# One layer of graph aggregation, linear attention and routed delta-rule memory: two placement constants of the vector engine's row loop, 7 and 8, become 5 and 7

## The chip, the cores and the metric

One core of a Trainium2 chip runs the whole layer. The metric is the device time of one execution in microseconds (us), lower is better. Engines are named as in the profile: PE (TensorE), DVE (VectorE), ACT (ScalarE), POOL (GpSimd) and SP (SyncE, which here only issues DMAs).

## The reference, cut to what matters

The layer adds a graph convolution and a linear attention to x (1250 tokens x 512), and then a third part, to which the change belongs. It sends each token to two of four experts and runs a gated delta-rule recurrence over each expert's tokens:

```
scores = softmax(h @ Wgate); rw, sel = top_k(scores, 2)     # 4 experts
q = l2norm(silu(h @ Wq)); k = l2norm(silu(h @ Wk)); v = silu(h @ Wv)   # 8 heads x 64
beta = sigmoid(h @ Wb)
g = -exp(A_log) * softplus(h @ Wa + dt_bias)
# per expert, over its tokens in order:
S = S * exp(g_t); kv = k_t S; delta = (v_t - kv) * beta_t
S = S + k_t (x) delta;  o_t = (q_t * scale) S
core = sum over the two experts of rw * o
out = (rmsnorm(core) * silu(h @ Wg)) @ Wo
```

## The kernel before, in words

Tokens are cut into 10 tiles of 125 (`NT = 10`). Each token takes part twice, which makes 2500 slots, padded to 2560 and cut into 40 chunks of 64; two chunks are one unit of the recurrence (20 units). The change lies in the stage before the recurrence, the feature stage, from some 380 to 510 us of the trace. What happens there, engine by engine, each in the order of its own program:

- **PE** projects each token tile three times, for q, k and v (`project_rows(t, w)`, w = 0, 1, 2, L783; 8 matmul instructions a projection), t from 0 to 9. Before projection (t, w) it waits until ACT has taken (t-1, w) out of the same bank. After the three projections of tile `DECAY_AT` it runs `decay_sums()` (L827 to L834): three transposes and two sums over the gates `gbg`, for which it waits on `gb_ready`. After tile 9 come the gate projections of tiles 1 to 4 (w = 3), then `features(0)` (L869), the first transposes of the recurrence, which wait for q and k rows of unit 0 from memory; then `head_gate(5)` (L994).
- **ACT** takes each projection out with SiLU (L1128 for w = 0 and 1, L1130 for w = 2). Behind (t+1, 0) it takes the square roots of tile t (`row_norms`, L1171), for which it waits on `ss_done` from DVE. SiLU, Sqrt and Exp each need a table load when they follow one another. After tile `DECAY_AT` it runs `decays()` (L1157 to L1167), the exponentials of what `decay_sums()` made.
- **DVE** runs the loop over tiles that the constants belong to. `squares(t)` (L1903 to L1905) waits for ACT's (t, 1), and sets `ss_done`; `unit_rows(t)` (L1911 to L1914) waits for the square roots and for (t, 2), and sets `rows_done`. After tile `GAMMA_AT` comes `gates_in()` (L1877 to L1885): it waits on `gb_loaded`, copies the gates into `gbg` (which sets `gb_ready`) and beta into `bet`. After tile `DECAY_AT` comes `decay_rows()` (L1887 to L1894), which turns ACT's exponentials into `stepT`, `gamT` and `bdec`, and sets `rows_made` and `scal_done`.
- **POOL** sends 20 scatters of the gates to `gb_slots` (L1385), then two scatters for each tile of q, k and v rows to `qkv_slots` (L1391), each behind `rows_done` of its tile. A row is 6144 bytes.
- **SP** waits until all gate scatters have landed, loads the gates back as `gbp` (L454, two DMAs; each row of a chunk is 64 bytes), then waits on `rows_made`, writes `stepT` and `gamT` to memory (L458, L459), waits until they have landed, and issues eight loads from them for units 0 and 1 (L465). Only then does it wait for the last row scatters and issue the loads of q and k for units 0 and 1 (L481).

`gb_loaded` reaches its 32 when both loads of `gbp` have landed in full.

Of the kernel before, what the change touches and what calls it, by code (L numbers as in the profile page):

```python
# [46 lines left out]
LB = NT // 2  # L47
GROUPS = ((0, 5), (5, 10), (0, 4), (4, 8), (8, 10))
XR = 112
GAMMA_AT = 7  # L50
DECAY_AT = 8
EARLY = 5
LATE = 7
ROOTS_BEHIND = {(2, 2): 0, (3, 0): 1, (3, 2): 2, **{(t, 0): t - 1 for t in range(4, NT)}}
# [48 lines left out]
def gps_layer(nc, d, out):  # L103
# [5 lines left out]
    with ctx:  # L109
# [430 lines left out]
        def _(pe):  # L540
# [233 lines left out]
            def project_rows(t, w, tiles=()):  # L774
                b0 = feature_bank(t, w)
                if w < 3 and t:
                    pe.wait_ge(S["f_act"], feature_count(t - 1, w))
                if w == 3 and 1 <= t < 4:
                    pe.wait_ge(S["f_act"], feature_count(NT - 1, t - 1))
                if w == 3 and t >= 4:  # L780
                    pe.wait_ge(S["f_act"], feature_count(t - 4, 3))
                for k in range(KC):
                    last = mm(bank[:, b0, :], xT[:, k, t * P:t * P + 128], W[:, w, k, :], start=(k == 0), stop=(k == KC - 1))  # L783
                    if k == KC - 1:
                        last.then_inc(S["f_psum"], 1)
                    if tiles:
                        for i in range(2):
                            small = token_logits(tiles[k // 2], k % 2 * 2 + i)
                if NT - 1 in tiles:
                    small.then_inc(S["logit_psum"], 1)  # L790
# [36 lines left out]
            def decay_sums():  # L827
                pe.wait_ge(S["gb_ready"], 1)
                for g in range(3):
                    c0, c1 = 16 * g, min(16 * g + 16, NCK)  # L830
                    last = nc.tensor.transpose(bank[0:(c1 - c0) * H, 6, g * CL:(g + 1) * CL], gbg[0:CL, c0 * H:c1 * H], ident[0:CL, 0:CL])
                last.then_inc(S["decay_psum"], 1)
                mm(bank[:, 7, 0:NCK * H], later, gbg[:, :], start=True, stop=True)
                mm(bank[:, 0, 0:NCK * H], alike, gbg[:, :], start=True, stop=True).then_inc(S["decay_psum"], 1)  # L834

            for t in range(2, NT):
                for w in range(3):
                    project_rows(t, w)
                if t == DECAY_AT:
                    decay_sums()  # L840
# [223 lines left out]
        def _(act):  # L1064
# [92 lines left out]
            def decays():  # L1157
                act.wait_ge(S["decay_psum"], 1)
                act.wait_ge(S["step_exp"], 1)
                A(stepT[:, 0:2, :], bank[:, 6, 0:2 * CL].rearrange("p (g n) -> p g n", g=2), ACT.Exp)  # L1160
                A(stepT[0:64, 2, :], bank[0:64, 6, 2 * CL:3 * CL], ACT.Exp).then_inc(S["step_exp"], 1)
                act.wait_ge(S["decay_psum"], 2)
                for b0, to in ((7, bdec), (0, gtot)):
                    for b in range(2):
                        q = slice(CL * b, CL * b + CL)
                        last = A(to[q, :, :], bank[q, b0, 0:NCK * H].rearrange("p (c b j) -> p b c j", b=2, j=HB)[:, b], ACT.Exp)
                last.then_inc(S["decay_exp"], 1)  # L1167

            def row_norms(t):
                act.wait_ge(S["ss_done"], t + 1)  # L1170
                A(nrm[:, t % 4, :], nrm[:, t % 4, :], ACT.Sqrt).then_inc(S["rn_done"], 1)  # L1171
# [6 lines left out]
            for t in range(2, NT):  # L1178
                for w in range(3):
                    feature_rows(t, w)  # L1180
                    if (t, w) in ROOTS_BEHIND:
                        row_norms(ROOTS_BEHIND[t, w])
                if t == DECAY_AT:
                    decays()
# [315 lines left out]
        def _(dve):  # L1500
# [375 lines left out]
            def gates_in():  # L1876
                dve.wait_ge(S["gb_loaded"], 32)  # L1877
                for b in range(2):
                    last = V.tensor_copy(gbg[:, :].rearrange("p (c b j) -> p b c j", b=2, j=HB)[:, b],
                                         gbp[:, :, 0:H].rearrange("p c (j b) -> p b c j", b=2)[:, b])  # L1880
                last.then_inc(S["gb_ready"], 1)
                for b in range(2):
                    q = slice(CL * b, CL * b + CL)
                    step(V.tensor_copy(bet[q, :, :], gbp[q, :, H:2 * H].rearrange("p c (j b) -> p b c j", b=2)[:, b]))
                step(V.memset(headT[:, :, :], 0.0))  # L1885

            def decay_rows():  # L1887
                dve.wait_ge(S["step_exp"], 2)
                step(V.tensor_copy(headT[:, :, 0:1], stepT[:, :, 0:1]))
                V.memset(stepT[:, :, 0:1], 0.0).then_inc(S["rows_made"], 1)  # L1890
                dve.wait_ge(S["rows_made"], 1)
                V.tensor_tensor_scan(flat(gamT), flat(stepT), flat(headT), 0.0, ALU.mult, ALU.add).then_inc(S["rows_made"], 1)
                dve.wait_ge(S["decay_exp"], 1)
                V.tensor_tensor(bdec[:, :, :], bdec[:, :, :], bet[:, :, :], ALU.mult).then_inc(S["scal_done"], 1)  # L1894
# [12 lines left out]
            def unit_rows(t):  # L1907
                b = t % 4
                qk = row_tile(t)[:, 0:2 * D]
                dve.wait_ge(S["rn_done"], t + 1)  # L1910
                step(V.reciprocal(nrm[:, b, :], nrm[:, b, :]))  # L1911
                V.scalar_tensor_tensor(tt3(qk[:, 0:D]), tt3(qk[:, 0:D]), DH ** -0.5, bc(nrm[:, b, 0:H], DH), ALU.mult, ALU.mult)
                dve.wait_ge(S["f_act"], feature_count(t, 2))
                V.tensor_tensor(tt3(qk[:, D:2 * D]), tt3(qk[:, D:2 * D]), bc(nrm[:, b, H:2 * H], DH), ALU.mult).then_inc(S["rows_done"], 1)  # L1914
# [5 lines left out]
            for t in range(NT):  # L1920
                squares(t)
                unit_rows(t)
                if t == GAMMA_AT:
                    gates_in()
                if t == DECAY_AT:
                    decay_rows()
# [175 lines left out]
```

## Time and profile before

| | us |
|---|---|
| median of 3 runs | 882.66 (880.85 to 884.09) |
| the profiled execution, its own time | 880.85 |
| its span in the trace | 879.0 |
| PE busy | 811.3 (92%) |
| DVE busy | 641.8 (73%) |
| POOL busy | 340.4 (39%) |
| ACT busy | 311.7 (35%) |

The span runs from the first to the last instruction; 1.85 us of the profiled execution lie around it. All starts in the rows are microseconds from the span's start. A share of busy time is an average over stages with different limits, so what bounds one stage is read from the engines' timelines and the chain of waits in that stage.

### The profile page before, as it was taken

The page shows a single profiled execution, that of the slowest core. Times are in us where ns is not written, and L with a number is a line of the kernel's source. Part 1 is how long each engine was busy: PE and PEld are TensorE (multiplying, and loading weights), DVE is VectorE, ACT ScalarE, POOL GpSimd, SP SyncE. Part 2 cuts the span into 40 slices and gives each one's busy share as a digit, 9 for nine tenths or more (in the row PEclk, how much of TensorE's full clock was granted, in tenths as well). Part 3 has the DMA queues.
Part 4 walks back from the last instruction along what each step waited for, and adds up shares of the span by engine and source line. Part 5 has one row for each costly group of instructions (what it writes and reads, how often), then busy time and mean ns, then how long its engine had stood idle before and what let it go on. Part 6 is the DMA issues. An engine that isn't in the chain of part 4 may idle for free.

```text
span 879.0 us, 23079 instructions
## 1 busy us (share of the span) xinstructions
PE 811.3 (92%) x9754; PEld 546.6 (62%) x9754; DVE 641.8 (73%) x1345; ACT 311.7 (35%) x548; POOL 340.4 (39%) x300
## 2 busy tenths in 40 slices
PE   2998999999999999999999978999999999997698
PEld 2454444344566657765444447989889898887343
DVE  7999999986888755526844437888887877783385
ACT  1231112210222220033645533555556465553352
POOL 5221110000111140000772346878767777771550
PEclk9999999999999989999999998999999999999899
DMA  8500000031000034000059544454544544421462
GB/s 253 185 1 1 0 2 1 1 72 46 2 1 1 2 114 150 0 1 1 5 198 387 194 128 112 120 151 125 140 128 133 148 132 135 124 56 40 120 178 70
DMA packets 74958, 80.42 MB, mean 91 GB/s; under 512 B 34452, under 2 KB 57670, under 8 KB 74853
## 3 DMA queue, kind: packets, MB, share of 16 engines
q1 hardware_dynamic: 69733, 57.78, 23.5%
q0 software_dynamic: 5120, 21.14, 6.7%
q8 instruction: 79, 1.29, 0.6%
q14 instruction: 26, 0.21, 0.1%
HBM read 54.44 MB, written 24.39 MB: 90 GB/s over the span
## 4 chain that ended last, share of the span: by engine, by line
PE 69%; DVE 23%; issue 3%; DMA 2%; POOL 1%; ACT 1%; SPq 1%; DVEq 0%; POOLq 0%; ACTq 0%
PE bank L783 12%; PE bank L852 8%; PE bank L878 4%; PE bank L1051 4%; PE bank L593 4%; DVE rows L1551 4%; PE bank L579 4%; PE bank L904 3%; DVE rows L1553 3%; PE bank L799 3%; DVE rows L1680 3%; PE bank L800 3%; PE bank L952 3%; PE bank L939 2%; PE bank L869 2%
## 5 line engine op out<-in xcount | busy, mean ns | idle before, releaser
L783 PE MATMUL bank<-W,xT 128*128 128x512 f32 x280 | 124.0, 596 | 0.0
L783 PEld LDWEIGHTS bank<-W,xT 128*128 128x128 f32 x280 | 52.0, 190 | 59.3 <-issue 58.4
L1371 POOL TENSOR_TENSOR cnt_r<-cnt_r,ident_sb 125x125 fp32r<-125x125 f32 x10 | 11.4, 1139 | 173.9 <-ACT cnt_r L1116 173.9
L557 PE MATMUL bank<-W,xT 128*125 128x512 f32 x160 | 77.1, 596 | 0.0
L579 PEld LDWEIGHTS bank<-rows 128*126 128x126 f16 x360 | 43.5, 135 | 34.7 <-issue 24.2
L1686 DVE TENSOR_SCALAR rows<-iota_sb,tC 128x625 f16<-128x625 f16 x180 | 56.2, 378 | 10.5 <-PE bank L579 10.5
L579 PE MATMUL bank<-rows 128*126 128x313 f16 x360 | 58.9, 299 | 4.2 <-DVE rows L1686 4.1
L1551 DVE TENSOR_SCALAR rows<-iota_sb,gbp 125x180 f16<-125x180 f16 x160 | 56.3, 352 | 0.0
L1553 DVE TENSOR_SCALAR rows<-iota_sb,gbp 125x180 f16<-125x180 f16 x160 | 50.4, 315 | 0.0
L567 PE MATMUL bank<-rows 125*128 125x360 f16 x160 | 42.7, 318 | 5.7 <-DVE rows L1553 3.3
L852 PE MATMUL bank<-big 64*64 64x64 f32 (+1 forms) x1280 | 43.8, 212 | 3.1 <-issue 2.0
L557 PEld LDWEIGHTS bank<-W,xT 128*125 128x125 f32 x160 | 28.9, 190 | 25.6 <-issue 25.0
L799 PE MATMUL bank<-hs_high,cnt_r 125*125 125x512 f32 x100 | 42.6, 426 | 1.3 <-DVE hs_r L1788 1.3
L1220 ACT ACTIVATE tB<-bank 128x1024 f16<-128x1024 f32 x40 | 40.9, 1023 | 7.1 <-PE bank L904 5.4
L646 PE MATMUL bank<-xT,W 128*128 128x500 f32 (+1 forms) x96 | 42.1, 520 | 1.3 <-ACT W L1105 0.7
L567 PEld LDWEIGHTS bank<-rows 125*128 125x128 f16 x160 | 15.4, 96 | 43.9 <-DVE rows L1553 29.3
L976 PE MATMUL bank<-state,W 64*64 64x64 f32 x640 | 42.1, 224 | 0.1
L980 PE MATMUL bank<-tC,W 64*64 64x64 f32 x640 | 41.0, 221 | 0.4 <-issue 0.4
L712 PE MATMUL bank<-W,xT 128*125 128x512 f32 x80 | 40.8, 591 | 0.0
L852 PEld LDWEIGHTS bank<-big 64*64 64x64 f32 (+1 forms) x1280 | 39.0, 128 | 2.8 <-issue 1.8
L800 PE MATMUL bank<-hs_r,cnt_r 125*125 125x512 f32 x100 | 40.3, 403 | 0.0
L1070 ACT ACTIVATE xT<-bank 128x500 f32<-128x500 f32 x20 | 11.0, 587 | 82.1 <-PE bank L551 82.1
(338 smaller groups left out, 1976.8 us busy)
## 6 DMA issues: line engine op xcount, KB each, us to landing
big<-qkv_slots SPq DMA_DIRECT2D x40, 256.0 KB, 3.5
rows<-step_rows SPq DMA_DIRECT2D x40, 128.0 KB, 3.2
rows<-gam_rows SPq DMA_DIRECT2D x40, 128.0 KB, 3.3
big<-qkv_slots SPq DMA_DIRECT2D x80, 64.0 KB, 2.8
big<-qkv_slots SPq DMA_DIRECT2D x40, 128.0 KB, 2.9
o_slots<-big SPq DMA_DIRECT2D x40, 128.0 KB, 2.8
x_all<-in_x SPq DMA_DIRECT2D x10, 224.0 KB
out<-tC SPq DMA_DIRECT2D x10, 224.0 KB
```

The lines of the kernel that those rows point to most:

```text
L557: last = mm(dst, xT[:, k, t * P:(t + 1) * P], W[:, w, k, :], start=(k == 0), stop=(k == KC - 1 and bias is None))
L567: mm(bank[:, 7, 0:2 * SW], oh_row[:, i // SB % SR, i % SB, :], oh_col[:, i % (SR * SB), :, :].rearrange("p a n -> p (a n)"), start=False, ...
L579: last = mm(bank[0:OW, b0 + k, 0:n], oh_src[:, g % 2, j, :], oh_dst[:, i % WB, t0:t0 + n], start=(j == 0), stop=(j == SC - 1))
L646: last = mm(bank[:, u % 2, 0:n], W[:, 2, k, c * 128:(c + 1) * 128], xT[:, k, t0:t0 + n], start=(k == 0), stop=(k == KC - 1))
L783: last = mm(bank[:, b0, :], xT[:, k, t * P:t * P + 128], W[:, w, k, :], start=(k == 0), stop=(k == KC - 1))
L799: mm(bank[0:P, t % 2, :], cnt12[:, s, t * P:(t + 1) * P], hs_high[:, s, :], start=(s == 0), stop=False)
L800: last = mm(bank[0:P, t % 2, :], cnt12[:, s, t * P:(t + 1) * P], hs_low[:, s, :], start=False, stop=(s == NT - 1))
L852: last = mm(bank[q, b0, a * CL:(a + 1) * CL], lhsT[q, a, :], rhs[q, a, :], start=start(a), stop=True, skip_group_check=not start(1))
L976: mm(bank[q, DB, o0 + j * DH:o0 + (j + 1) * DH], qG[u // 2 % 2][u % 2][q, c2 * HB + j, :], state[q, c % 2, j, :], start=True, stop=False)
L1551: V.tensor_scalar(oh_col[:, i % (SR * SB), 0, :], iota[0:P, 0:SW], e_col[:, i:i + 1], e_src[:, i:i + 1], ALU.is_equal, ALU.mult)
L1553: V.tensor_scalar(oh_col[:, i % (SR * SB), 1, :], iota[0:P, 0:SW], e_col[:, i:i + 1], e_dst[:, i:i + 1], ALU.is_equal, ALU.mult).then_inc( ...
L1686: V.tensor_scalar(oh_dst[:, i % WB, :], iota[:, 0:HN], srt[:, 1, i:i + 1], None, ALU.is_equal).then_inc(S["onehots_done"], 1)
```

## The change

Two constants. `gates_in()` on DVE moves from behind tile 7 to behind tile 5. `decay_sums()` on PE, `decays()` on ACT and `decay_rows()` on DVE, which share the other constant, move from behind tile 8 to behind tile 7. Nothing is added or removed.

```diff
-GAMMA_AT = 7
-DECAY_AT = 8
+GAMMA_AT = 5
+DECAY_AT = 7
```

## Rows read from the trace of the kernel before

**Rows 1.** Chain of waits, 380 to 560 us: start us, duration us, what, count.
```profile
408.88 72.25 PE bank L783 x168
481.13 0.32 PE bank L831 x3
...
482.73 10.31 PE bank L783 x24
...
498.34 6.39 DMA qkv_slots<-big,posi
...
505.19 4.76 DMA big<-qkv_slots
...
510.08 1.64 PE bank L869 x8
```

**Rows 2.** Timeline of DVE: start us, duration us, engine, line, operation.
```profile
456.68 0.68 DVE L1914 TENSOR_TENSOR big<-big,nrm 128x512 f32<-128x512 f32 x1
...
477.96 0.39 DVE L1879 COPY gbg<-gbp 128x160 f32<-128x160 f32 x2
...
479.12 1.23 DVE L1903 TENSOR_TENSOR tB<-big 128x1024 f32<-128x1024 f32 x1
...
481.64 0.17 DVE L1905 TENSOR_SCALAR nrm<-nrm 128x16 f32<-128x16 f32 x1
```

**Rows 3.** Timeline of SP, the DMAs it issues.
```profile
449.12 5.07 SPq L454 DMA_DIRECT2D gbp<-gb_slots  x2
490.83 0.41 SPq L458 DMA_DIRECT2D step_rows<-stepT  x1
...
497.28 3.43 SPq L465 DMA_DIRECT2D rows<-step_rows  x4
```

**Rows 4.** DMA queues, 448 to 454.6 us: packets, MB, share of 16 engines.
```profile
q1 hardware_dynamic: 2565, 0.16, 26.7%
```

**Rows 5.** DMA queues, 454.6 to 474 us.
```profile
q0 software_dynamic: 1450, 7.93, 98.7%
q1 hardware_dynamic: 1232, 0.08, 4.4%
```

**Rows 6.** DMA queues, 474 to 475.5 us.
```profile
q0 software_dynamic: 76, 0.37, 63.1%
q1 hardware_dynamic: 1036, 0.07, 47.4%
```

**Rows 7.** DMA queues, 475.5 to 477 us.
```profile
q1 hardware_dynamic: 319, 0.02, 14.6%
```

**Rows 8.** DMA queues, 477 to 484.5 us.
```profile
q0 software_dynamic: 452, 2.43, 79.3%
```

**Rows 9.** Timeline of POOL: the first scatter of tile 6, the second of tile 7.
```profile
470.99 0.95 POOL L1391 DMA_INDIRECT qkv_slots<-big,posi  x1 [7.48 <-DVE big L1914]
...
479.62 1.55 POOL L1391 DMA_INDIRECT qkv_slots<-big,posi  x1 [0.30 <-issue]
```

**Rows 10.** Timeline of ACT, tile 7's root to projection (8, 1).
```profile
476.21 0.22 ACT L1171 ACTIVATE nrm<-nrm 128x16 f32<-128x16 f32 x1
476.44 1.28 ACT L1128 ACT_TABLE_LOAD   x1
477.74 0.60 ACT L1128 ACTIVATE big<-bank 128x512 f32<-128x512 f32 x1
...
484.60 1.28 ACT L1128 ACT_TABLE_LOAD   x1
```

**Rows 11.** Timeline of PE: both head gates.
```profile
511.51 4.75 PE L994 MATMUL bank<-W,xT 128*128 128x512 f32 x8
...
517.88 3.60 PE L994 MATMUL bank<-W,xT 128*128 128x512 f32 x8
```

**Rows 12.** Busy by window: us, each engine's busy (instructions), PEclk, DMA share, GB/s.
```profile
484.00:490.00 6.00, 6.00 (x16) 2.65 (x15) 1.61 (x4) 5.59 (x8) 0.00 (x0) 1.00 0.00 0
...
511.50:516.30 4.80, 4.80 (x12) 2.18 (x11) 0.00 (x0) 1.09 (x3) 3.87 (x3) 0.76 0.02 3
```

## The prediction

> **What bounds the kernel now.** I read the chain of waits first. From 408.88 us it stays on PE through 21 projections without a gap (168 matmuls in 72.25 us, 3.44 us a projection), then `decay_sums()` from 481.13, then the last three projections from 482.73 to 493.04 [rows 1]. So the feature stage is bound by PE, and whatever makes PE wait there is paid in full. Behind it the chain leaves PE: ACT takes (9, 2) out, tile 9's roots and rows follow, POOL issues the last scatter at 498.34, it lands 6.39 us later, the q and k loads take 4.76 us, and at 510.08 the recurrence begins [rows 1]. That tail hangs on the end of projection (9, 2), so a shift of 493.04 shifts the start of the recurrence, and all behind it, by nearly the same.
>
> Second, the timeline of DVE, to see what room each moved piece has. `unit_rows(5)` ends at 457.36, `gates_in()` starts at 477.96 [rows 2]. The change moves `gates_in()` to 457.4: some 20 us earlier, in an engine that runs its program in order.
>
> Third, because `gates_in()` waits for a DMA, the DMA queues over time. SP issues both loads of `gbp` from 449.12 to 454.19 and nothing more until 490.83 [rows 3], so every packet of the hardware queue in between is theirs. 2565 of them go by 454.6 [rows 4]; then only 1232 in 19.4 us, beside 1450 packets of the software queue that carry 7.93 MB and keep the 16 engines 98.7% busy [rows 5]. These are POOL's row scatters for tiles 0 to 5, two a tile, issued before 463.5 [rows 9]. At 474 they run out: 1036 small packets go in 1.5 us, the last 319 before 477.0, and none after it [rows 6 to 8]. The sum is 5152, both loads. The second load, of 160 KB, therefore takes from 454 to about 477, because it shares each engine nearly packet by packet with 6 KB packets. It landed less than 1 us before DVE asked for it at 477.96. The place of `gates_in()` is just late enough in the kernel before.
>
> **The change part by part.**
>
> *Work moved.* `gates_in()` takes 1.16 us (477.96 to 479.12) [rows 2], `decay_sums()` 1.60 us (481.13 to 482.73) [rows 1], `decays()` on ACT 2.8 us (from the end of taking out (8, 2), 481.13 + 0.02 + 0.60, to the SiLU table load at 484.60) [rows 1, 10]. All run once before and once after, with the same table loads: 0 by themselves. No DMA is added.
>
> *The new wait.* Call T the time at which `gb_loaded` is complete. The loads are issued at the same time as before and meet the same 12 scatters, whose issue ended 7.48 us ahead of 470.99 [rows 9]. Tile 6's scatters, which began at 470.99 and so took part of the last 3 us, now come behind `gates_in()`, so T can come a little earlier: bounds 475.5 and 477.0 [rows 6, 7], and I take 476.0. DVE stands from 457.4 to 476.0, 18.6 us. Behind the wait on DVE are `squares(6)`, `unit_rows(6)` and all later tiles; ACT waits for `ss_done` of tile 6 at its root, in front of (7, 1); PE waits for `gb_ready` after (7, 2), which it ends at 481.13 less three projections, 470.81.
>
> *When PE can start (8, 1).* Two paths. Through ACT: T, `gates_in()` 1.16, `squares(6)` 2.69 (479.12 to 481.81) [rows 2], 0.2 to pass it on, root 0.23, SiLU table 1.28, taking out (7, 1) 0.60 [rows 10]: T + 6.2. Through PE: `gbg` copied at T + 0.4, `decay_sums()` 1.60, projection (8, 0) 3.44: T + 5.4 at full clock. PE will have stood idle for 5.6 us. The only like case near it: after PE's idle time before 510.08 the granted clock was 0.76 over 511.5 to 516.3 [rows 12], part at full (2.4 GHz) and part at half (1.2 GHz); the eight transposes there took 1.64 us [rows 1] and eight matmuls 4.75, against 3.60 later for the same eight [rows 11]. The matmuls alone lost 1.15; scaling the transposes by the same share gives 0.4 to 0.6 more. So the clock costs 0 to 1.7 and I take 1.7, as this idle time is longer: T + 7.1, which is 483.1. The Trainium skill, TensorE: Matmul & The Clock Gate, section "What's actually happening", has the engine at 1.2 GHz once it has stood idle, which speaks for the full loss; a stall in the middle of the projections, where this matters, no row here shows. If the clock stayed up, the path through ACT would decide, and the sum would be 0.9 less.
>
> *From there.* Before, (8, 1) started at 481.13 - 2 x 3.44 = 474.25. After it come five projections in the changed kernel, 17.2 us, with `decay_sums()` already done: 483.1 + 17.2 = 500.3 for the end of (9, 2), against 493.04: +7.3. ACT keeps up on the same durations: (7, 2) is out at about 482.8 and PE needs it at 486.5; `decays()` ends at 485.6, then a SiLU table and (8, 0) to 487.5, needed at 490.0; root 7 between two table loads, then (8, 1) to 490.9, needed at 493.4.
>
> *What comes late next.* `decay_rows()` now waits for `unit_rows(7)`, which hangs on root 7 at 488.9, so `rows_made` comes at about 491.5, against 490.83 when SP saw it before [rows 3]: no earlier, though its place is one tile earlier. SP issues the eight row loads from some 498 to 505, as before [rows 3], while the last scatter is issued at 498.34 + 7.3 = 505.6. So these loads no longer run beside the last scatter. It took 6.39 us [rows 1]; one with no other traffic, issued at 479.62, was done by 484.5 [rows 8, 9, 12], 4.9. The relief is 0 to 1.5 there, 0 to 0.5 on the q and k loads; I take 1.1 together. PE's four gate projections end at 500.3 + 13.8 = 514.1, ahead of `features(0)` at 510.1 + 6.2 = 516.3.
>
> *Sum.* +7.3 - 1.1 = +6.2 us. On the profiled execution's own time 880.85 + 6.2 = 887.1 (its span 885.2, with 1.85 around it). The median of the runs shown is 1.8 above that execution, so the forecast for a median is 882.7 + 6.2 = 888.9. The mechanism's own bounds: T at 475.5, no clock loss, full relief: 475.5 + 6.2 + 17.2 = 498.9, +5.9 - 2.0 = +3.9, and a further 1.4 off if the shorter idle time before `features(0)` leaves the clock up: +2.5. At the top T at 477.0, clock loss, no relief: +8.3.
>
> **The rivals.**
>
> *A, the load is there early and the earlier decays pay (faster).* If T were 469.7 or less, PE would find `gbg` and (7, 1) in time (470.81 + 1.60 + 3.44 = 475.85, less 6.2): that is the point from which it decides. Then `rows_made` comes at about 480, the writes and the eight row loads are done before the last scatter, which lands in 4.9 instead of 6.39 us, and the q and k loads gain up to 0.5: -2.0, and -1.0 more if PE, idle for 1.3 us instead of 3.3, keeps its clock: about -3.0, 879.7. For it: the first load went at some 500 packets a microsecond [rows 4]. Against it: the second at 64 [rows 5], in the very traffic that stays. The Trainium skill, DMA: Bandwidth & Descriptors, section "Queues, rings and completion order", has an engine drain a whole packet of some 9 to 17 descriptors from one ring before it turns to another. With nine small ones to each large one, T would be some 3 us after 454.6 and this rival would win; the rows count 1232 against 1450, about one to one, and they decide. 5%.
>
> *B, the wait is there but swallowed (no change).* PE is idle before 510.08 for 3.3 us, and a pause in the middle could be made up there. For it: that idle time, and the lighter DMA traffic behind it. Against it: the idle time is the end of a chain that itself starts at (9, 2), so it moves with the stall; only relief and clock, 3.4 at most, come off. If also the path through PE cost less than I think: +2, 884.7. 12%.
>
> *C, the stall is dearer.* Tiles 6 and 7 now scatter at 483 and 491 and the last three tiles' traffic is as dense as before; if the load in 475.5 to 477 is not helped, T at 477.0 (+1.0), the clock low for twice as long (+1.7), and nothing relieved (7.3 in place of 6.2): +10, 892.7. 8%.
>
> **How the numbers follow.** The forecast has 75%. A measurement of this kernel can tell about 0.5% (4.4 us) from no change. In the forecast's own case the shift is over 4.4 in five of six, which with C gives 0.71 for slower; B, the low end of the forecast's case and a little of A give 0.24 for the same; A the rest, 0.05. The range from 884.0 (+1.3, most of B) to 892.0 (+9.3, part of C) leaves out A and the rest of C, some 15% with the spread of the runs, 3.2 us, on top.
>
> **What would show it right or wrong.** Right: DVE idle for 18 to 20 us before L1879, released by the DMA of `gbp`, which starts there near 476; PE idle for 5 to 6 us before L831 near 476.5; the granted clock low for a few microseconds from there; (9, 2) taken out at about 500; the last scatter shorter than 6.39 us; `features(0)` at about 516. Wrong: L1879 starting before 470 (A), or PE's gap small; `features(0)` within 2 us of 510 (B); the clock loss missing takes 0.9 off. If the hardware queue's 64-byte packets between 454.6 and 474 are not near 1200 again, my reading of how the load shares the engines is wrong.

## The result and the profile after

The changed kernel takes 887.43 us in the median of 5 (887.12 to 888.31), the kernel before 882.42 (880.85 to 884.09; two executions more than were shown before the prediction). The ratio is 1.0069, with a 95% interval of 1.0044 to 1.0095; it is not the quotient of the two medians (1.0057). How it was formed isn't recorded; over all 24 executions on record of the changed kernel the median is 887.58 and the quotient of the means 1.0070. So the changed kernel is slower by 5 us going by the medians and by 6 going by the ratio (3.9 to 8.4): under 1%, but clear of the noise. 888.9 had been forecast.

The timeline of DVE in the changed kernel answers to [rows 2]: start, duration, engine, line, operation, and in brackets the idle time before it and what ended that.

```profile
456.80 0.68 DVE L1914 TENSOR_TENSOR big<-big,nrm 128x512 f32<-128x512 f32 x1
476.42 0.40 DVE L1879 COPY gbg<-gbp 128x160 f32<-128x160 f32 x2 [18.93 <-DMA gbp<-gb_slots]
...
477.59 1.23 DVE L1903 TENSOR_TENSOR tB<-big 128x1024 f32<-128x1024 f32 x1
...
480.10 0.17 DVE L1905 TENSOR_SCALAR nrm<-nrm 128x16 f32<-128x16 f32 x1
```

DVE stands still for 18.93 us, and the load of `gbp` ends that. The DMA queues from 454.6 to 474 us show the same traffic as [rows 5]: packets, MB, share of 16 engines.

```profile
q0 software_dynamic: 1459, 7.98, 99.1%
q1 hardware_dynamic: 1205, 0.08, 4.3%
```

The timeline of PE shows its stall, and the windows below it the clock (busy time and instructions of each engine, PEclk as a share of 2.4 GHz, DMA share, GB/s):

```profile
439.81 31.06 PE L783 MATMUL bank<-W,xT 128*128 128x512 f32 x72
476.87 0.58 PE L831 MATMUL bank<-ident_sb,gbg 64*128 64x64 f32 x3 [5.99 <-DVE gbg L1879]
...
479.67 35.88 PE L783 MATMUL bank<-W,xT 128*128 128x512 f32 x80
516.23 1.10 PE L869 MATMUL bank<-ident_sb,big 128*128 128x128 f32 x8 [0.69 <-ACT hs L1133]
517.16 3.60 PE L994 MATMUL bank<-W,xT 128*128 128x512 f32 x8
```

```profile
470.90:476.80 5.90, 0.00 (x0) 0.00 (x0) 0.38 (x3) 0.00 (x0) 0.00 (x0) 0.90 0.84 287
476.80:482.40 5.60, 5.53 (x11) 3.03 (x12) 4.78 (x10) 2.06 (x4) 0.00 (x0) 0.50 0.00 0
482.40:488.10 5.70, 5.70 (x15) 2.59 (x14) 2.62 (x3) 5.59 (x12) 1.90 (x2) 1.00 0.69 276
```

PE idles 5.99 us. The clock is full up to 475.6, in the middle of the idle time, and 0.50, which is 1.2 GHz, from there to 482.4. ACT and POOL, for the end of the stage:

```profile
481.84 0.60 ACT L1128 ACTIVATE big<-bank 128x512 f32<-128x512 f32 x1
...
501.85 0.60 ACT L1130 ACTIVATE big<-bank 128x512 f32<-128x512 f32 x1 [2.83 <-PE bank L783]
...
515.58 0.60 ACT L1133 ACTIVATE hs<-bank 125x512 f32<-125x512 f32 x1 [2.84 <-PE bank L783]
```

```profile
507.12 0.95 POOL L1391 DMA_INDIRECT qkv_slots<-big,posi  x1 [0.30 <-issue]
```

(9, 2) is taken out at 501.85, 8.8 us later than 493.04 [rows 1], `features(0)` starts at 516.23, 6.15 later, and it is no longer held by a DMA but by PE's own gate projections and ACT behind them (L1133). Last, SP:

```profile
449.23 5.04 SPq L454 DMA_DIRECT2D gbp<-gb_slots  x2
491.67 0.41 SPq L458 DMA_DIRECT2D step_rows<-stepT  x1
...
512.28 1.77 SPq L481 DMA_DIRECT2D big<-qkv_slots  x4
```

`rows_made` comes 0.84 us later than before [rows 3], although its place is one tile earlier. The last scatter is over when SP goes on, 512.28 - 507.12 = 5.2 us after its issue, against 6.39 [rows 1].

**A measure for the rest.** Executions of one kernel start this stage up to 1.8 us apart, and their recurrences differ by more. So I compare profiled executions by the time from SP's issue of L454 to PE's first key product (L878, the first work of the recurrence that needs all of unit 0's features): "stage" below. Before: 516.10 - 449.12 = 67.0 us (PE's L878 starts at 516.10). After: 520.60 - 449.23 = 71.4, +4.4. The rest of the trace, L878 to the first L1051, took 317.9 us in the profiled execution before and 322.2 in the one after; over the 14 profiled executions of this case it lies anywhere from 317.9 to 324.1. That is why the profiled execution after (890.02 us) is 9.2 us above the one before while the medians are 5.0 apart. The same kernel in e7 has 319.1, so most of it is spread between executions; whether the change also adds a little there is not shown.

### The profile page after: what moved, and what is told of

It reads as the page before. It is cut to its first block, busy times and chain, and to the rows that moved or that the text cites. A ratio compares the mean times of both kernels' runs of the same rounds, so it can differ in the third digit from the quotient of the medians.

```text
span 888.2 us, 23079 instructions
## 1 busy us (share of the span) xinstructions
PE 813.3 (92%) x9754; PEld 548.2 (62%) x9754; DVE 643.9 (72%) x1345; ACT 312.0 (35%) x548; POOL 339.9 (38%) x300
## 4 chain that ended last, share of the span: by engine, by line
PE 62%; DVE 23%; issue 5%; DMA 4%; POOL 4%; ACT 1%; SPq 1%; DVEq 0%; POOLq 0%; ACTq 0%
PE bank L852 8%; PE bank L783 6%; PE bank L878 4%; PE bank L1051 4%; PE bank L579 4%; DVE rows L1551 3%; PE bank L904 3%; PE bank L593 3%; DMA gbp<-gb_slots 3%; PE bank L799 3%; DVE rows L1680 3%; PE bank L952 3%; DVE rows L1553 3%; PE bank L800 3%; PE bank L939 2%
## 5 line engine op out<-in xcount | busy, mean ns | idle before, releaser
L852 PE MATMUL bank<-big 64*64 64x64 f32 (+1 forms) x1280 | 45.6, 217 | 2.5 <-issue 1.9
L852 PEld LDWEIGHTS bank<-big 64*64 64x64 f32 (+1 forms) x1280 | 40.8, 133 | 2.6 <-issue 2.1
```

What stands on the lines that cost most here:

```text
L852: last = mm(bank[q, b0, a * CL:(a + 1) * CL], lhsT[q, a, :], rhs[q, a, :], start=start(a), stop=True, skip_group_check=not start(1))
```

## The experiments

Every kernel was timed against the kernel before on its chip. The ratio's 95% interval stands in brackets; the ratio can lie 0.001 beside the quotient of the two medians, and where the two differ the interval is what counts. No kernel is more than 1.1% from the kernel before.

| kernel | median | before | ratio | stage |
|---|---|---|---|---|
| before | 882.42 | | | 67.0 |
| after | 887.43 | 882.42 | 1.0069 [1.0044, 1.0095] | 71.4 |
| e7, after again | 887.00 | 882.61 | 1.0040 [1.0022, 1.0058] | 71.3 |
| e1, 5 and 8 | 892.29 | 882.19 | 1.0108 [1.0078, 1.0138] | 77.3 |
| e6, 6 and 7 | 888.28 | 882.61 | 1.0060 [1.0037, 1.0083] | 72.3 |
| e5, 6 and 8 | 885.28 | 882.61 | 1.0028 [1.0004, 1.0052] | 66.9 |
| e11, 6 and 8 again | 887.46 | 880.74 | 1.0073 [1.0049, 1.0097] | 69.6 |
| e2, load first, 5 and 7 | 879.59 | 882.19 | 0.9963 [0.9944, 0.9983] | 62.6 |
| e8, load first, 5 and 6 | 879.48 | 882.61 | 0.9952 [0.9935, 0.9970] | 62.6 |
| e3, load first, 7 and 8 | 882.41 | 882.19 | 0.9998 [0.9977, 1.0020] | 66.2 |
| e4, clock kept, 5 and 7 | 888.68 | 882.19 | 1.0071 [1.0043, 1.0099] | 70.4 |
| e10, clock kept, q and k first, 5 and 7 | 886.32 | 880.74 | 1.0060 [1.0039, 1.0082] | 69.5 |
| e9, q and k first, 7 and 8 | 877.88 | 880.74 | 0.9963 [0.9947, 0.9978] | 62.7 |
| e12, both, 5 and 7 | 877.69 | 883.29 | 0.9934 [0.9918, 0.9950] | 62.6 |

### Is it the slow load?

```diff
                 gates_out(t)
+            pool.wait_ge(S["gb_loaded"], 32)
             for t in range(NT):
                 rows_out(t)
```

> The changed constants (5 and 7), and POOL waits until both loads of gbp have landed before it issues the first scatter of q, k and v rows. My theory: the load was slow only because its 64-byte packets took turns with 6 KB packets. Alone it lands at about 456.5 instead of 476.4, so DVE doesn't wait, PE goes through to (9, 2) at about 493.0, and the scatters, which start 8 us late, have caught up before tile 8's. rows_made at about 480 instead of 491.7, the eight row loads are done before the last scatter; that takes 5 us instead of 6.4 and the q and k loads 3.4 instead of 5; features(0) at about 507.5 against 510.1 before, the clock stays up behind it: 2.6 to 4.2 us less than before, 878 to 880 us. Rival: the load is slow by itself (2560 packets of 64 bytes in its second half), and lands at 476 also without company: then the scatters start at 476, 20 us late, ACT waits at (8, 0) for the first scatters, and the time is over 895 us.

> The constants of before (7 and 8) with the same wait of POOL for the loads of gbp. It tells what the wait does by itself. My theory: gates_in() did not wait before either, rows_made stays at 490.8, and the tail behind (9, 2) is as before: 882.4 us, within 1. Rival: the order of the transfers alone brings what the kernel with 5 and 7 gains: 878 to 880 us. Another: scatters that start 8 us late cost time: 884 or more.

With 5 and 7 it took 879.59 us, 2.6 less than before; with 7 and 8 it took 882.41, the same as before. The DMA queues of e2 from 448 to 456 us (packets, MB, share), then its SP and PE:

```profile
q1 hardware_dynamic: 5152, 0.33, 42.8%
q0 software_dynamic: 64, 0.02, 1.0%
```

```profile
450.22 2.38 SPq L454 DMA_DIRECT2D gbp<-gb_slots  x2
481.56 0.40 SPq L458 DMA_DIRECT2D step_rows<-stepT  x1
```

```profile
471.79 0.39 PE L831 MATMUL bank<-ident_sb,gbg 64*128 64x64 f32 x3
...
508.47 1.09 PE L869 MATMUL bank<-ident_sb,big 128*128 128x128 f32 x8 [0.69 <-ACT hs L1133]
```

All 5152 packets of the two loads go by 456 us instead of 476 to 477, in the same form; only the company is gone. Even the issue takes 2.38 us instead of 5.04. POOL stands 6.7 us ahead of its first scatter, but neither DVE nor PE waits for the load, and `rows_made` comes 10 us earlier. So the rival that calls the load slow by itself is out. e3 says that POOL's wait alone gives nothing measurable in the time, and 0.8 us in the stage. The fair comparison for the places alone is therefore e2 with e3: 62.6 against 66.2, a gain of 3.6 us of stage (2.8 in the medians) once their input is there in time, where without POOL's wait they cost 4.4.

### Which of the two constants, and which path

```diff
 e1: GAMMA_AT = 5, DECAY_AT = 8     e6: GAMMA_AT = 6, DECAY_AT = 7
 e5 and e11: GAMMA_AT = 6, DECAY_AT = 8
```

> GAMMA_AT = 5, DECAY_AT stays 8. My theory: the stall comes from DVE's wait for the load of gbp, whoever is behind it. DVE again waits from 457.5 to about 476.4. PE has no decay_sums() to wait for after (7, 2), runs (8, 0) to 474.3 and then waits for ACT's (7, 1), out at 476.4 + 6.2 = 482.6; the clock falls in between, so (8, 1) to (8, 2) lose 1 to 2 us more; decay_sums() 1.6 us still lies ahead. End of (9, 2): 482.6 + 17.2 + 1.6 + 1 to 2 = 502.4 to 503.4, against 493.0 before and 501.8 in the changed kernel. rows_made comes after unit_rows(8), so the row loads run beside the last scatter and there is no relief: features(0) 7 to 9 us later than before. Expected 889 to 891 us. Rival: the loss came from PE's wait in decay_sums() alone, and the gates' early place costs nothing: 882.4 us.

> GAMMA_AT = 6, DECAY_AT = 7. Tile 6's squares and root are done before DVE's wait, so ACT has (7, 1) out in time, and only PE's wait for gb_ready in decay_sums() is left, with T as in the changed kernel. My theory: in the changed kernel the path through PE decided ((8, 1) started at 484.7, (7, 1) was out at 482.4), so this kernel stalls PE as long, 470.9 to 476.9 and the clock behind it, and (9, 2) ends at 501 to 502: 887 us, as the changed kernel. Rival: the path through ACT (roots behind squares(6)) decided, and here the stall is 2 us or more shorter: 885 or less.

e1 took 892.29 us, dearer than the whole change and a little over the range expected. The gates' place alone makes the stall, through ACT:

```profile
477.51 0.40 DVE gbg L1879 x2
...
481.64 1.28 ACT L1128
482.93 0.01 issue
482.94 0.61 ACT big L1128
483.55 0.04 issue
483.59 9.57 PE bank L783 x16
```

This is e1's chain of waits. PE starts (8, 1) at 483.59, after 8.2 us of idle time, and its first two projections take 9.57 us, against 6.88 at 3.44 each. In e1 `decay_rows()` follows tile 8, so the row loads run beside the last scatter again, which takes 6.35 us by the chain of waits. Moving the decays too, as the change does, was worth 6 us of stage against that.

e6 took 888.28, a little over the 887 expected. The lines of DVE and PE that carry its reading:

```profile
477.76 0.39 DVE L1879 COPY gbg<-gbp 128x160 f32<-128x160 f32 x2 [6.60 <-DMA gbp<-gb_slots]
478.21 0.58 PE L831 MATMUL bank<-ident_sb,gbg 64*128 64x64 f32 x3 [6.93 <-DVE gbg L1879]
```

DVE waits only 6.60 us instead of 18.93. Tile 6's root is not late there, so the path through ACT is out. PE stands 6.93 us instead of 5.99, because the load lands 28.2 us after its issue instead of 27.2, and the stage is 0.9 us longer. In the changed kernel, too, (7, 1) was out at 481.84 + 0.60 = 482.4, and PE needed it at 484.7. PE's wait for `gb_ready` and the clock decide, and the length of DVE's wait does not.

### What the clock costs

```diff
             def decay_sums():
+                for _ in range(24):
+                    mm(bank[:, 6, :], zeros16[:, 0:128], zeros16[:, :], start=True, stop=True)
                 pe.wait_ge(S["gb_ready"], 1)
```

> The changed kernel (5 and 7), with 24 fp16 matmuls of 128x512 on zeros into the unused bank 6 ahead of PE's wait for gb_ready: PE is busy in place of idle for about 5.2 of the 6.0 us. My theory: the granted clock stays at full, decay_sums() takes 1.6 us instead of 3.0 and (8, 0) 3.4 instead of 4.8; (8, 1) then starts when (7, 1) is out, near 482.6 instead of 484.7, so (9, 2) ends near 499.7 instead of 501.8: 2 us less than the changed kernel, 885.3 us. Rival: the clock had no part in it, the path through ACT decides: 887.4 us.

It took 888.68 us: the expectation of 885.3 was wrong. The stage shows the part that was right. PE's and POOL's timelines and the windows of e4 (lines from L829 on are two further down):

```profile
471.49 5.34 PE L829 MATMUL bank<-zeros 125*128 125x512 f16 x24
477.70 0.39 PE L833 MATMUL bank<-ident_sb,gbg 64*128 64x64 f32 x3 [0.87 <-DVE gbg L1881]
...
483.32 31.17 PE L783 MATMUL bank<-W,xT 128*128 128x512 f32 x72 [0.53 <-ACT big L1130]
...
516.11 1.06 PE L871 MATMUL bank<-ident_sb,big 128*128 128x128 f32 x8 [1.62 <-DMA big<-qkv_slots]
```

```profile
477.70:483.30 5.60, 5.10 (x15) 2.43 (x15) 4.71 (x9) 2.12 (x4) 0.05 (x1) 1.00 0.00 0
```

The clock stays at 1.00, and (8, 1) starts 6.1 us after the load's end instead of 8.2 (484.65 - 476.42), now held by ACT. (9, 2) comes out at 500.80 where the whole stage started 0.8 us late: 1.8 us gained. But SP issues the row loads later, 50.5 us after L454 instead of 48.9, so they run beside the last scatter again. That takes 6.52 us instead of 5.2, PE waits for the q and k loads, and the stage ends 0.9 us earlier, not 2. The chain of waits of e4:

```profile
506.06 6.52 DMA qkv_slots<-big,posi
...
513.04 2.93 DMA big<-qkv_slots
```

> The changed constants (5 and 7), the 24 matmuls on zeros ahead of PE's wait, and the same order of SP's loads. With the 24 matmuls alone the end of (9, 2) came 1.9 us earlier, but the last scatter took 6.6 us beside the row loads instead of 5.1 and features(0) came no earlier. My theory: the clock's share of the stall was only hidden by the tail. Without that traffic features(0) follows PE's gate projections, 2 us earlier than in the changed kernel: 885 us. Rival: the clock's share is not worth anything at the end, whatever the tail: 887 to 889.

With SP's order changed as below, the stage of e10 is 69.5, 1.9 us under the changed kernel's, and `features(0)` is held by PE's gate projections again. That agrees with the 1.8 us measured at (9, 2), so the clock's two microseconds are there in the stage; no run has the new order with 5 and 7 and without the 24 matmuls, so the order's own share is argued, not shown. They did not reach the medians: 5.6 us above before in e10 and 6.5 in e4, against 5.0 and 4.4 for the changed kernel, with intervals that overlap. In the profiled executions what lies behind the stage took 324.1 us in e4, the most of all 14, and 321.7 in e10, against 322.2 and 319.1 for the changed kernel. Whether the added matmuls cost something there or this is spread stays open, and with it whether keeping the clock is worth anything in the end.

### The traffic beside the last scatter

```diff
-            for s in range(2):
-                load_rows(arow[s], step_rows, s, arow_loaded[s])
-            for s in range(2):
-                load_rows(grow[s], gam_rows, s, grow_loaded[s])
+            load_rows(arow[0], step_rows, 0, arow_loaded[0])
             ...
                 for w in (1, 0):
                     load_qk(s, w)
+            load_rows(grow[0], gam_rows, 0, grow_loaded[0])
+            load_rows(arow[1], step_rows, 1, arow_loaded[1])
+            load_rows(grow[1], gam_rows, 1, grow_loaded[1])
```

> The constants of before (7 and 8). SP issues only unit 0's step rows ahead of its wait for the last row scatters, then the q and k loads, and the other six row loads (unit 0's gam rows first) behind them. It takes out the traffic beside the last scatter and the q and k loads, and nothing else. My theory: that traffic is what the first of the two gains of the kernel with 5 and 7 behind POOL's wait consisted of. The last scatter lands in about 5.1 us instead of 6.4, q and k in 3.5 instead of 5, features(0) at 507.4 to 508 instead of 510.1, held by PE's gates and ACT, and the clock stays up: 879.6 us, 2 to 3 below before. Rival: the scatter and the loads are as slow without company (their own 6 KB packets), or the row loads are now late for POOL's decayed_keys(0): 882.4 or more.

It took 877.88 us, 2.9 under before, with the constants of before: as expected. The timelines of SP and PE in e9:

```profile
496.74 1.29 SPq L465 DMA_DIRECT2D rows<-step_rows  x2
503.47 1.77 SPq L481 DMA_DIRECT2D big<-qkv_slots  x4
```

```profile
506.98 1.06 PE L869 MATMUL bank<-ident_sb,big 128*128 128x128 f32 x8 [0.76 <-ACT hs L1133]
507.88 3.60 PE L994 MATMUL bank<-W,xT 128*128 128x512 f32 x8
```

PE no longer waits for a DMA (in the kernel before it stood from 506.8 to 510.08), and its clock stays up: eight matmuls in 3.60 us instead of 4.75 [rows 11].

> POOL's wait for the loads of gbp with GAMMA_AT = 5 and DECAY_AT = 6. With 5 and 7 features(0) was already held by PE's gate projections and ACT behind them, not by a transfer, so row loads that are done one tile earlier have nothing left to shorten. My theory: as with 5 and 7, 879.6 us, within 1. Rival: the row loads still cost the last scatters or the q and k loads something, and a tile earlier brings 1 us or more: 878.5 or less. Another: the writes of stepT and gamT now fall into the backlog of scatters; they land later but nothing waits: no loss.

> The changed constants (5 and 7), POOL's wait for the loads of gbp, and SP's new order (unit 0's step rows, then q and k, then the other row loads). Each alone ended at features(0) held by PE's gate projections and ACT's last one. My theory: both took out the same traffic from the same tail, so they don't add up: the gain of one, 2.5 to 3 us below before, stage and time as with either. Rival: they add up, 5 us or more below before. Another: with the row loads behind q and k although they were ready 10 us before, something in unit 0 is late, and it is slower than either.

Both came out as expected in the stage: 62.6 with either remedy, with both, and with the decays a tile earlier still, since the gate projections now hold `features(0)`. e12's ratio of 0.9934 is better than either's, but its own 877.69 us equals e9's 877.88, and the kernel before ran slower on that chip. Whether the two add anything is not settled; the stage says no. e2, e8, e9 and e12 all beat both kernels of this case, by 0.4 to 0.7% against the kernel before.

### On the near side of the turning point

> GAMMA_AT = 6, DECAY_AT = 8. It stands on the near side of the point from which the wait decides. My theory: DVE waits before gates_in() too, from about 470.7 to 476.5, some 6 us, but what is behind it has room: squares(7) ends at 480.4, ACT has (8, 1) out at about 482.5, and PE needs that bank for (9, 1) only at 486.2; decay_sums() finds gb_ready. PE does not wait and (9, 2) ends at 493: 882.3 us, within 1. Rival: any wait of DVE at gates_in() is paid, since DVE feeds roots and scatters in order: 882.3 + 6 = 888.

> GAMMA_AT = 6, DECAY_AT = 8 once more. The first time PE stood nowhere for it in the profiled execution (881.8 us), but the median was 885.3 with executions from 880.2 to 888.3, where the kernel before lies between 879 and 886. Still my theory: the wait has some 3 us of room, so an execution in which the load of gbp lands late or ACT has one of its odd pauses can lose a few us, most lose none: 882 to 885 us, wider spread than before. Rival: a fixed cost of 2.7 us that the first profile does not show: 885.3 again.

The expectation failed, twice: 885.28 and 887.46 us. In the first profiled execution nothing was lost, in the second 2.7 us of stage. The two timelines of DVE, e5 first, then e11, and e11's chain of waits:

```profile
478.37 0.40 DVE L1879 COPY gbg<-gbp 128x160 f32<-128x160 f32 x2 [6.29 <-DMA gbp<-gb_slots]
```

```profile
479.97 0.39 DVE L1879 COPY gbg<-gbp 128x160 f32<-128x160 f32 x2 [12.39 <-DMA gbp<-gb_slots]
```

```profile
495.23 0.40 SPq L458
...
501.70 0.63 SPq L465
...
508.22 0.53 SPq L481
508.80 3.75 DMA big<-qkv_slots
...
512.68 1.94 PE bank L869 x8
```

From the issue of L454 the load takes 28.0 us in e5 (478.37 - 450.37) and 31.0 in e11 (479.97 - 449.02). The difference is tile 6's scatters. In e5, as in the profiled execution before, ACT pauses ahead of (6, 2):

```profile
467.86 0.60 ACT L1130 ACTIVATE big<-bank 128x512 f32<-128x512 f32 x1 [8.95 <-remote]
```

In e11 it doesn't, and tile 6's scatters follow the first 12 without a gap (467.85 in place of 472.37), so the load shares its engines with 14 scatters, 3 us longer. The same is seen with 7 and 8 in e9, which up to this point is the kernel before: its DVE waits at L1879 as well.

```profile
479.64 0.54 DVE L1879 COPY gbg<-gbp 128x160 f32<-128x160 f32 x2 [2.14 <-DMA gbp<-gb_slots]
```

In e11 PE still loses next to nothing, but tiles 7 to 9 are late on DVE, `rows_made` comes at 495.2, and SP's row loads, in order in front of the q and k loads, are not all issued before 508.1: a path that my turning point of 469.7 us, worked out from PE alone, left out. e5 is already on it. Its chain of waits goes the same way, SP comes to the q and k loads at 506.55, and from DVE's copy of the gates to `features(0)` it is 32.9 us there (478.37 to 511.25) and 32.7 in e11 (479.97 to 512.68). By these two traces, each microsecond by which the load lands later with 6 and 8 moves the recurrence by one, and e5's stage equals that of before only because its load came early enough. The kernel before was close to this path as well: SP had issued its last row load at 504.37 and went on at 504.75, when the scatter was over. Why ACT pauses in some executions (before, e5, e6, e7) and not in others, the trace does not say: as what ended the pause it gives `remote`, and names no engine and no queue. Nor do two traces explain the medians. The profiled executions of e5 (881.76 us) and e11 (883.34) are among the fastest of their kernels, and the slowest of the others took 6.5 and 6.2 us more; no trace shows one of those.

> The changed kernel again, beside the others on one chip: 887.4 us by its first timing. Its profiled execution was 2.6 us above that median, all of it gathered in the recurrence; here the start of the recurrence should again be 6 us later than before, and the whole 4 to 6 us.

887.00 us, 4.4 above before, and the stage +4.3: the changed kernel repeats.

## Why the prediction was right, point by point

- **What bounds it.** Right for both kernels of this case: PE's run of projections, and what follows (9, 2). That SP's row loads were only 0.4 us from holding the tail themselves I had not seen; it did not matter here, but it is where e11's stage lost its 2.7 us.
- **T, the landing of `gbp`.** 476.0 forecast, 476.4 measured; DVE's wait 18.6 and 18.93 us. In the five kernels with 5 and the shared traffic (after, e7, e1, e4, e10) DVE goes on 27.1 to 27.3 us after the issue of L454. e2 shows the cause. What I had wrong is how the kernel before stands: its last packets pass between 476.6 and 477.0, so the load landed 1.0 to 1.4 us before DVE asked for it, not less than 1, and that only where ACT had paused; without the pause DVE waits 2.1 us there too (e9). The constants of before were not just late enough, they had no margin.
- **Path through ACT.** T + 6.2 forecast, 482.4 - 476.4 = 6.0 measured.
- **Path through PE.** Its sum was mis-sized in one term, the clock: 1.7 us assumed. `decay_sums()` took 3.0 us (476.87 to 479.88) instead of 1.6, and (8, 0) ended at 484.7 (501.85 less five projections) instead of 483.3: 2.8 together. The low clock lasted 5.5 us of PE's work, 476.9 to 482.4. In the stretch that I scaled from it was 0.50 from 511 to 513 and between 0.59 and 0.68 in the windows beside that, which comes to 3.4 us. (8, 1) started at T + 8.2, not T + 7.1. That PE's path and not ACT's decides was right (e6, e4).
- **End of (9, 2).** +7.3 forecast, +8.8 measured: 0.4 from T, 1.1 from the clock.
- **What comes late next.** `rows_made` at about 491.5 forecast, 491.67 seen by SP. The relief was right in kind and too small (and the scatter of 4.9 us that I measured it by was not alone: the window of [rows 8] holds 2.43 MB, three scatters' worth): 1.1 us taken, but the scatter alone gained 1.2, and scatter and loads together at least 2.6 (8.8 less 6.15), since they no longer held PE at 516.23. PE's gate projections, which I had 2.2 us ahead, came last. `features(0)` at +6.15 against +6.2 is luck: two errors cancelled.
- **Behind `features(0)`.** I had put the clock's recovery there (1.4 us) only into the lower bound. It came in full: eight matmuls in 3.60 instead of 4.75 us, first key product +4.5. The median's +5.0 is the stage's +4.4 within the noise, and so is the ratio's +6.1. With this term in the sum the forecast would have been about 887.5.
- **The rivals.** A did not happen in the changed kernel, but e2 is A, made to happen: -4.4 in the stage, -2.6 in the median, where I had priced -3.0. The interval of its ratio goes from -4.9 to -1.5 us, so it is not shown that part of what the stage wins fails to reach the end. A's "some 3 us" for nine small packets a turn is 3.8 by the same rows (2587 packets, 75 large ones a microsecond), which changes nothing. B named the right places where something is given back, relief and clock, and put them at 3.4 us at most; they gave 4.4 (8.8 at (9, 2), 4.4 at the first key product), half of the stall, but no more. C's longer low clock did come in part (+1.1 of its +1.7), with 0.4 of its 1.0 in T, and the relief it denied came too.

## What to carry to other kernels

Before a wait is moved forward in an in-order engine, find when its input lands, and what the transfer shares its engines with: here two loads of 160 KB each, in 64-byte packets, took 27 us together, because beside the 6 KB packets of the scatters they got through about one small packet for each large one (1205 to 1459), and the same loads took under 6 us alone. Follow every engine behind the wait, also the one that only issues DMAs: with 6 and 8 it was SP's row loads, and not PE, that passed the wait on. If the input is late, order the transfers first (here one wait, on the engine that issues the scatters, turned +5 us into -2.6), and move the work afterwards. And price a stall with what it takes along: PE's idle time of 6 us was followed by a loss of 2.8 us at the low clock, and at least 2.6 came back where the stall pulled two transfers apart.

## What the runs showed of the hardware

- A load beside large packets also holds the issuing engine longer: L454's two DMAs took SP 5.0 to 5.2 us to issue beside the scatters and 2.3 to 2.4 us without them (e2, e3, e8, e12).
- After 5.99 us without a matmul PE ran at 1.2 GHz all through 476.8 to 482.4, at work; `decay_sums()` and (8, 0) took 7.8 us instead of 5.0. In e1, with 8.2 us of idle time, two projections took 2.7 us longer (9.57 instead of 6.88): a third more idle time cost no more clock.
- ACT stood for 8.8 to 9.0 us ahead of (6, 2) in 4 of 14 profiled executions. In the kernel before its input was ready 6 us before it went on (PE was through at 460.5, ACT began at 466.48). Two shorter stops of this kind, 2.0 and 3.1 us, are in e8. As what ended them the trace gives only `remote`.
